# Second layer norm of an adaLN block: normalised rows of groups 1 to 7 on ScalarE instead of GpSimd

## The chip, the core and the metric

The kernel runs on one core of a Trainium2 chip. The core has five instruction streams: TensorE (PE, matmuls and transposes into PSUM banks), VectorE (DVE), ScalarE (ACT), GpSimd (POOL, which cannot read PSUM) and SyncE (SP, which issues the DMAs here). Each runs its own program in order; they wait for one another by semaphores. The metric is device time of one execution in microseconds, the median of several runs.

## The reference

One transformer block on x of 2 x 2048 rows of 512, in float32:

```python
h = _layernorm(x) * (1 + ca) + sa
x = x + ga * attn(h)          # 16 heads, linear attention: elu(q)+1, elu(k)+1, o_w
h = _layernorm(x) * (1 + cb) + sb
x = x + gb * ffn(h)           # gate, up: 512 -> 1376, silu(gate) * up, down: 1376 -> 512
```

with `_layernorm(x) = (x - mean) / sqrt(var + 1e-5)` over the 512 columns; ca, sa, ga, cb, sb, gb come from a small modulation product, and the three weights of the feed-forward part are looked up in a table of 16 values by index matrices. The part that the change touches is the second `_layernorm(x)`.

## The kernel before, in words

The 4096 rows are cut into 8 groups of 512 (4 tiles of 128 rows). Every large product runs as three float16 matmuls on a high and a low part of each operand (the helper `three`, lines 1128 to 1130).

The first half (to about 400 us) runs the first layer norm, the projections and the key-value sums over all groups. The second half is `stage_b(s)` for s = 0 to 7, on each engine in its own function of that name. Stage s runs the gate and up products of the feed-forward part, one chunk (slot) of 128 of the 1376 columns after the other: 9 slots in stage 0, 11 in stage 1, 13 in stage 2, 11 later. Between the slots it runs the attention output and the second layer norm of group n = s + 1, and it starts the attention of group n + 1. After stage 7 come the down products (from about 960 us), which don't concern us.

One slot goes round all engines: TensorE's gate matmuls (12), ScalarE's `silu_gate` (line 707), TensorE's up matmuls (12), VectorE's `hid_full` (line 1062, needs silu and up), ScalarE's `hid_hi` (line 714, the float16 high part), GpSimd's `hid_lo` (line 539, the low part), and a DMA to memory. TensorE's gate of a slot waits for the silu of two slots before, its up for the `hid_full` of two slots before.

The second layer norm of group n: `x1_tile` on VectorE adds the attention output and takes the statistics of a tile; GpSimd's `xn_b` waits for the four statistics and computes 1/sqrt(var + eps) and -mean/sqrt(var + eps) in four short instructions (`norm`, lines 454 to 460), then the normalised rows of the four tiles (line 511) into `xn2`, part of the tile called arena; TensorE transposes them (`t_piece`, line 1136); ScalarE's `h_b` scales and shifts the result into h2 (lines 583, 584), and GpSimd's `h_lo_b` (line 516) makes its low part. Group 0 of the second norm runs in the first half, with its own tile.

The attention of group n + 1 needs a denominator: TensorE's `z_sum` (line 1249), ScalarE's `den` (line 655, a copy of the bank to `kb_row`), VectorE's `rec` (line 1002, the reciprocal), TensorE's `z_spread` (line 1266), VectorE's `qn_full` (line 1009).

The order of all this is written out by hand: each engine's `stage_b` has two tables, `before` and `after`, that say what runs ahead of and behind the slot's own instruction (on ScalarE ahead of and behind `hid_hi`, on GpSimd of `hid_lo`, on VectorE of `hid_full`). VectorE also runs the table lookups of the weights (lines 885 to 893) in the gaps, up to stage 5.

The semaphores that matter: `nmr2_done` counts GpSimd's chain, `xn2_done` the normalised rows (SyncE's `x_next` and TensorE's `t_piece` wait for it), `x2T_done` the transposes.

Of the kernel before, what the change touches and what calls it, by code (L numbers as in the profile page):

```python
# [26 lines left out]
ACT = mybir.ActivationFunctionType  # L27
# [15 lines left out]
TILES = GROUP // P  # L43
# [51 lines left out]
def adaln_kernel(nc, x, qwT, qb, kwT, kb, vwT, vb, owT, ob, lut, gateT, upT, downT, cT, wmod, out):  # L95
    with ExitStack() as ctx:
        def sb(name, shape, dt):
            return ctx.enter_context(nc.sbuf_tensor(name, shape, dt))
# [4 lines left out]
        def part(arena, start, dt, *dims):  # L103

            n = 1
            for d in dims:
                n *= d
            words = n * (2 if dt == F16 else 4) // 4
            v = arena[:, start:start + words]
            if dt != U32:  # L110
                v = v.bitcast(dt)
            if len(dims) == 2:
                v = v.rearrange("p (a b) -> p a b", a=dims[0])
            elif len(dims) == 3:
                v = v.rearrange("p (a b c) -> p a b c", a=dims[0], b=dims[1])
            elif len(dims) == 4:
                v = v.rearrange("p (a b c d) -> p a b c d", a=dims[0], b=dims[1], c=dims[2])
            return v
# [10 lines left out]
        xn2 = part(arena, 2 * tile_w, F32, TILES, HID)  # L129
# [19 lines left out]
        xg = sb("xg", [P, 2, TILES, HID], F32)  # L149
# [49 lines left out]
        ve, rstd, nmr, half, qb_col, qb_neg = (sc[:, SC_ALL + i * TILES:SC_ALL + (i + 1) * TILES] for i in range(6))  # L199
# [11 lines left out]
        def sems(names):  # L211
            return (sem(n) for n in names.split())
# [27 lines left out]
        o_done, xob_done, x1_done, stats2_raw, stats2_done, ve2_done, rstd2_done, nmr2_done, xn2_done = sems(  # L240
            "o_done xob_done x1_done stats2_raw stats2_done ve2_done rstd2_done nmr2_done xn2_done")
        x2T_done, h2_f_done, h2_done = sems("x2T_done h2_f_done h2_done")
# [30 lines left out]
        def wait_apart(eng, s, n):  # L273

            eng.wait_ge(s, n)
            eng.sem_inc(waited, 1)

        def run(extra, at):

            for piece in extra.get(at, ()):  # L280
                piece()
# [158 lines left out]
        def _(pool):  # L440
# [10 lines left out]
            def norm(n, ready, s_ve, s_rstd, s_nmr):  # L451

                wait_apart(pool, ready, 4 * n + 4)
                pool.tensor_scalar(ve, mv[:, :, 1], 1.0, LN_EPS, ALU.mult, ALU.add).then_inc(s_ve, 1)  # L454
                pool.wait_ge(s_ve, n + 1)
                pool.tensor_tensor(rstd, ve, half, ALU.pow).then_inc(s_rstd, 1)
                wait_apart(pool, s_rstd, n + 1)
                pool.tensor_scalar(nmr, mv[:, :, 0], -1.0, 0.0, ALU.mult, ALU.add).then_inc(s_nmr, 1)
                pool.wait_ge(s_nmr, 2 * n + 3)
                pool.tensor_tensor(nmr, nmr, rstd, ALU.mult).then_inc(s_nmr, 1)  # L460
                wait_apart(pool, s_nmr, 2 * n + 4)
# [43 lines left out]

            def xn_b(n, par, rows):
                wait_apart(pool, xn_done, 4 * GROUPS)
                norm(n, stats2_done, ve2_done, rstd2_done, nmr2_done)
                wait_apart(pool, x2T_done, 4 * n + 4)
                for t in range(TILES):  # L510
                    pool.tensor_scalar(rows[:, t], xg[:, par, t], rstd[:, t:t + 1], nmr[:, t:t + 1],
                                       ALU.mult, ALU.add).then_inc(xn2_done, 1)
# [14 lines left out]
            for g in range(6):  # L527
                stage_a(g, g % 2, True, {4: [clear_tail]} if g == 1 else {})

            stage_a(6, 0, True, {2: [lambda: xob(0, 0)], 6: [lambda: qn_lo(0, 0), lambda: qn_lo(0, 1)],  # L530
                                 7: [lambda: qn_lo(0, 2), lambda: qn_lo(0, 3)]}, M_LATE)
            stage_a(7, 1, False, {7: [lambda: xn_b(0, 0, xn2_of[0])]})
            for c in range(KC):
                h_lo_b(0, c)
# [32 lines left out]
            for g in range(GROUPS):  # L567
                par = g % 2
# [7 lines left out]
        def _(act):  # L576
# [4 lines left out]
            def h_chunk(dst, c, h_f_sem, scale, bias):  # L581

                act.activation(dst[:, 0, c], bank[c % 2][:], ACT.Identity, bias=bias, scale=scale)  # L583
                act.activation(h_f[:, c % 2], bank[c % 2][:], ACT.Identity, bias=bias, scale=scale).then_inc(h_f_sem, 1)  # L584
# [56 lines left out]
            def qs_all(n):  # L641
                q = q_of[n]
                act.wait_ge(q_in, 16 * (n + 1))
                for c in range(KC):
                    act.activation(q[:, c], q[:, c], ACT.Copy,
                                   scale=ksq[:, bass.ds(n // PER_BATCH, 1), c]).then_inc(qs_done, 1)

            def den(n):

                act.wait_ge(z_done, n + 1)  # L650
                if n == 1:
                    act.wait_ge(k_read, 4 * GROUPS)
                elif n:
                    act.wait_ge(spread_done, 4 * n)
                act.activation(z_rec[n], bank[6 if n else 1][:], ACT.Copy, bias=ATTN_EPS / SEQ).then_inc(z_read, 1)

            def qn_hi(n, c):
                act.wait_ge(qn_f_done, 4 * n + c + 1)
                if c == 0:
                    act.wait_ge(o_done, 4 * n + 4)  # L660
                act.activation(qn[:, 0, c], qn_f[:, c % 2], ACT.Copy).then_inc(qn_hi_done, 1)

            def h_b(n, c):
                b = n // PER_BATCH
                act.wait_ge(x2T_done, 4 * n + c + 5)
                act.wait_ge(h2_done, 4 * n + c + 3)
                if c == 0 and n >= H2S:
                    act.wait_ge(up_done, SLOT[(n - H2S, FC - 1)] + 1)
                h_chunk(h2[n % H2S], c, h2_f_done, modm[:, 2, c, bass.ds(b, 1)], modm[:, 3, c, bass.ds(b, 1)])
# [11 lines left out]
            for t in range(TILES):  # L681
                act.activation(xg[:, 0, t], xg[:, 0, t], ACT.Identity, bias=nmr[:, t:t + 1],
                               scale=rstd[:, t:t + 1]).then_inc(xn_done, 1)
# [15 lines left out]
            for c in range(KC):  # L699
                h_b(0, c)  # L700

            def silu_gate(e, j):
                m = rows_of(j)
                act.wait_ge(gate_done, e + 1)
                if e >= 2:
                    act.wait_ge(hid_f_done, e - 1)
                act.activation(silu_g[0:m, e % 2], bank[2 + 2 * (e % 2)][0:m], ACT.Silu, scale=c1(C_INV_G)[0:m]).then_inc(silu_g_done, 1)  # L707

            def hid_hi(e, j):
                m = rows_of(j)  # L710
                act.wait_ge(hid_f_done, e + 1)
                if e >= HIDS:
                    act.wait_ge(hid_out[e % HIDS], 16 * (e // HIDS))
                act.activation(hid[0:m, e % HIDS, 0], hid_f[0:m, e % 2], ACT.Copy).then_inc(hid_hi_done, 1)  # L714

            def stage_b(s):
                n = s + 1
                if s == 0:
                    before = {0: [lambda: den(1)], 2: [lambda: qn_hi(1, 0), lambda: qn_hi(1, 1)], 3: [lambda: qn_hi(1, 2), lambda: qn_hi(1, 3)],
                              6: [lambda: den(2)], 7: [lambda: h_b(1, 0), lambda: qn_hi(2, 0), lambda: qn_hi(2, 1)], 8: [lambda: h_b(1, 2)]}  # L720
                    after = {3: [lambda: qs_all(2)], 7: [lambda: h_b(1, 1)], 8: [lambda: h_b(1, 3), lambda: qn_hi(2, 2), lambda: qn_hi(2, 3)]}
                else:
                    before = {6: [lambda: h_b(n, 0)], 7: [lambda: h_b(n, 2)]}
                    after = {6: [lambda: h_b(n, 1)], 7: [lambda: h_b(n, 3)]}
                    if n + 1 < GROUPS:
                        before[1] = [lambda: qs_all(n + 1)]
                        before[4] = [lambda: den(n + 1)]
                        before[6] = [lambda: qn_hi(n + 1, 0), lambda: qn_hi(n + 1, 1), lambda: h_b(n, 0)]
                        before[7] = [lambda: qn_hi(n + 1, 2), lambda: qn_hi(n + 1, 3), lambda: h_b(n, 2)]
                for i, (g, j) in enumerate(STAGES[s]):  # L730
                    silu_gate(SLOT[(g, j)], j)
                    if n < GROUPS:
                        run(before, i)
                    hid_hi(SLOT[(g, j)], j)
                    if n < GROUPS:
                        run(after, i)

            for s in range(GROUPS):
                stage_b(s)
# [742 lines left out]
```

## Time and profile before

| | us |
|---|---|
| median of 3 timed runs | 1248.17 (1248.15 to 1250.17) |
| profiled execution | 1245.79 |
| its span, first to last instruction | 1244.0 |
| TensorE busy | 1163.0 (93%) |
| VectorE busy | 751.4 (60%) |
| ScalarE busy | 392.9 (32%) |
| GpSimd busy | 353.8 (28%) |
| mean granted TensorE clock | 0.979 of 2.4 GHz |

A row of a timeline reads: start, duration, engine, line, operation, output and inputs, shapes, how many in a row; in brackets how long the engine was idle before it and who ended that. Matmuls overlap: one of 512 columns is shown as 0.38 us, and the next starts 0.22 us behind it at 2.4 GHz and 0.43 us behind it at 1.2 GHz. The end of a run of matmuls is taken here as the last start plus 0.38 us.

### The profile page before, as it was taken

What the parts mean: (1) busy time and instruction counts of PE and PEld (TensorE: products, weight loads), DVE (VectorE), ACT (ScalarE), POOL (GpSimd) and SP (SyncE); (2) the same over time, 40 slices, a digit from 0 to 9 for tenths busy, and PEclk for the clock granted to TensorE, in tenths of its full rate; (3) what the DMA queues carried; (4) which work ended last, traced back from release to release, by engine and by line L of the source; (5) the groups of instructions that cost most, each with busy time, mean ns of one, the idle gap of its engine ahead of it and who ended that gap; (6) DMA issues with size and microseconds to landing.
All of it is one profiled execution on the core that took longest, in us unless ns stands there. A gap on an engine that the chain in (4) does not pass through costs nothing.

```text
span 1244.0 us, 14205 instructions
## 1 busy us (share of the span) xinstructions
PE 1163.0 (93%) x5462; PEld 543.5 (44%) x5462; DVE 751.4 (60%) x1105; ACT 392.9 (32%) x609; POOL 353.8 (28%) x337
## 2 busy tenths in 40 slices
PE   4689998899997987999999999999999999999998
PEld 1244444445544333444444444444444444444443
DVE  6897999998565478787786997957411110001000
ACT  3245556456546313242242432324142200000000
POOL 3101000000303426254372563726242211111211
PEclk8799999999999998999999999999999999999999
DMA  9902211221121441121221223112121324444441
GB/s 324 283 2 68 81 48 55 102 68 32 71 68 41 163 169 66 69 92 48 102 76 49 94 74 111 68 74 77 53 98 50 142 106 159 159 159 159 169 151 65
DMA packets 52229, 125.79 MB, mean 101 GB/s; under 512 B 5216, under 2 KB 15456, under 8 KB 47040
## 3 DMA queue, kind: packets, MB, share of 16 engines
q1 hardware_dynamic: 52160, 124.87, 28.9%
q8 instruction: 43, 0.70, 0.2%
q14 instruction: 26, 0.21, 0.1%
HBM read 77.15 MB, written 47.71 MB: 100 GB/s over the span
## 4 chain that ended last, share of the span: by engine, by line
PE 76%; DVE 12%; issue 6%; ACT 4%; POOL 1%; DMA 1%; SPq 0%; POOLq 0%; DVEq 0%; ACTq 0%
PE bank L1128 23%; PE bank L1129 23%; PE bank L1130 23%; DVE look_buf L893 3%; PE bank L1190 2%; PE bank L1136 1%; PE bank L1266 1%; DVE w_ffn L893 1%; PE bank L1308 1%; DMA w_ffn<-in_wmod 1%; ACT h L583 1%; DVE look_buf L890 1%; ACT h_f L584 1%; DVE shared L912 1%; PE bank L1249 1%
## 5 line engine op out<-in xcount | busy, mean ns | idle before, releaser
L1128 PE MATMUL bank<-h,w_ffn 128*128 128x512 f16 (+1 forms) x528 | 203.4, 385 | 13.9 <-POOL h L516 11.4
L1129 PE MATMUL bank<-h,w_ffn 128*128 128x512 f16 (+1 forms) x528 | 203.0, 385 | 0.0
L1130 PE MATMUL bank<-h,w_ffn 128*128 128x512 f16 (+1 forms) x528 | 202.8, 384 | 0.0
L539 POOL TENSOR_TENSOR shared<-hid_f,shared 128x512 f16<-128x512 f32 (+1 forms) x88 | 111.3, 1265 | 318.0 <-ACT shared L714 318.0
L1062 DVE SCALAR_TENSOR_TENSOR hid_f<-bank,sc,shared 128x512 f32<-128x512 f32 (+1 forms) x88 | 65.8, 748 | 150.2 <-PE bank L1130 114.9
L1069 DVE SCALAR_TENSOR_TENSOR shared<-bank,sc,gb_row 128x512 f32<-128x512 f32 x32 | 24.0, 751 | 215.6 <-PE bank L1130 215.6
L1128 PE MATMUL bank<-w_ffn 128*128 128x512 f16 (+1 forms) x352 | 136.3, 387 | 0.9 <-DVE hid_f L1062 0.9
L714 ACT ACTIVATE shared<-hid_f 128x512 f16<-128x512 f32 (+1 forms) x88 | 55.4, 630 | 257.4 <-DVE hid_f L1062 257.4
L1129 PE MATMUL bank<-w_ffn 128*128 128x512 f16 (+1 forms) x352 | 136.2, 387 | 0.0
L1130 PE MATMUL bank<-w_ffn 128*128 128x512 f16 (+1 forms) x352 | 136.2, 387 | 0.0
L1128 PE MATMUL bank<-arena,h 128*128 128x512 f16 x256 | 98.9, 386 | 6.6 <-issue 3.1
L707 ACT ACTIVATE shared<-bank,sc 128x512 f32<-128x512 f32 (+1 forms) x88 | 60.3, 685 | 130.4 <-PE bank L1130 130.3
L1130 PE MATMUL bank<-arena,h 128*128 128x512 f16 x256 | 98.8, 386 | 0.0
L1129 PE MATMUL bank<-arena,h 128*128 128x512 f16 x256 | 98.7, 385 | 0.0
L890 DVE TENSOR_SCALAR look_buf<-look_buf,tab_x,tab 128x512 uint32<-128x512 uint32 x133 | 97.7, 764 | 0.8
L572 POOL TENSOR_TENSOR xg<-xg,shared 128x512 f32<-128x512 f32 x32 | 40.9, 1278 | 198.2 <-DVE shared L1069 198.2
L1128 PEld LDWEIGHTS bank<-h,w_ffn 128*128 128x128 f16 (+1 forms) x528 | 53.5, 101 | 85.3 <-issue 17.8
L454 POOL TENSOR_SCALAR sc<-mv 128x4 f32<-128x4 f32 x16 | 5.5, 342 | 266.0 <-DVE mv L812 223.1
L1130 PEld LDWEIGHTS bank<-h,w_ffn 128*128 128x128 f16 (+1 forms) x528 | 53.6, 102 | 62.9 <-issue 3.3
L1129 PEld LDWEIGHTS bank<-h,w_ffn 128*128 128x128 f16 (+1 forms) x528 | 53.6, 101 | 59.0 <-issue 2.9
L893 DVE COPY_PREDICATED look_buf<-look_buf 128x512 uint32<-128x512 uint32 x76 | 73.2, 963 | 1.1
L1128 PE MATMUL bank<-arena,w_ffn 128*128 128x512 f16 (+1 forms) x176 | 66.8, 379 | 0.0
(189 smaller groups left out, 1994.3 us busy)
## 6 DMA issues: line engine op xcount, KB each, us to landing
hid_dram<-shared SPq DMA_DIRECT2D x80, 256.0 KB, 2.0
w_ffn<-hid_dram SPq DMA_DIRECT2D x8, 2560.0 KB, 9.6
xg<-in_x SPq DMA_DIRECT2D x16, 1024.0 KB, 6.9
qp_dram<-qp SPq DMA_DIRECT2D x8, 1024.0 KB, 4.9
x_dram<-xg SPq DMA_DIRECT2D x8, 1024.0 KB, 4.0
xg<-x_dram SPq DMA_DIRECT2D x8, 1024.0 KB, 5.0
out<-xg SPq DMA_DIRECT2D x7, 1024.0 KB, 11.1
qp<-qp_dram SPq DMA_DIRECT2D x6, 1024.0 KB, 5.2
```

Of the source, the lines that this page charges most:

```text
L539: pool.tensor_tensor(hid[0:m, e % HIDS, 1], hid_f[0:m, e % 2], hid[0:m, e % HIDS, 0], ALU.subtract).then_inc(hid_done, 1)
L572: pool.tensor_tensor(xg[:, par, t], xg[:, par, t], y_t[:, t % 2], ALU.add).then_inc(y_done, 1)
L707: act.activation(silu_g[0:m, e % 2], bank[2 + 2 * (e % 2)][0:m], ACT.Silu, scale=c1(C_INV_G)[0:m]).then_inc(silu_g_done, 1)
L714: act.activation(hid[0:m, e % HIDS, 0], hid_f[0:m, e % 2], ACT.Copy).then_inc(hid_hi_done, 1)
L890: ins = dve.tensor_scalar(buf(dst), buf("m0"), tab_x[:, a:a + 1], tab[:, 2 * a:2 * a + 1], ALU.bitwise_and, ALU.bitwise_xor)
L893: ins = dve.copy_predicated(buf(dst), buf(a), buf(b))
L1062: dve.scalar_tensor_tensor(hid_f[0:m, i], bank[3 + 2 * i][0:m], c1(C_HID)[0:m], silu_g[0:m, i], ALU.mult, ALU.mult).then_inc(hid_f_done, 1)
L1069: dve.scalar_tensor_tensor(y_t[:, t % 2], bank[2 + t][:], c1(C_INV_D), gb_row[:, g // PER_BATCH], ALU.mult, ALU.mult).then_inc(y_read, 1)
L1128: pe.matmul(dst, a_hi, b_hi, start=first, stop=False)
L1129: pe.matmul(dst, a_hi, b_lo, start=False, stop=False)
L1130: last = pe.matmul(dst, a_lo, b_hi, start=False, stop=end)
L1190: last = pe.matmul(bank[6 + c // 2][:, at:at + n], kp[:, t % 2, c * P:(c + 1) * P], v_one[:, t % 2, c], start=(t == 0 and c % 2 == 0), sto ...
```

## The change

The rows of groups 1 to 7 are no longer computed by GpSimd behind its `norm`, but by ScalarE, as activations with the function Identity, rstd as scale and nmr as bias. GpSimd keeps `norm` for all groups, and keeps the rows of group 0. ScalarE's new function waits for the chain (`nmr2_done`) and for the transposes of the group before (`x2T_done`). In stage 0 it stands behind `hid_hi` of slot 5, where GpSimd's stood behind `hid_lo` of slot 5. In stages 1 to 6 it stands behind `hid_hi` of slot 4; GpSimd's chain stays behind `hid_lo` of slot 3. GpSimd waits, ahead of `norm`, until ScalarE has read the factors of the group before.

```diff
@@ gpsimd
             def xn_b(n, par, rows):
                 wait_apart(pool, xn_done, 4 * GROUPS)
+                wait_apart(pool, xn2_done, 4 * n)
                 norm(n, stats2_done, ve2_done, rstd2_done, nmr2_done)
+                if n:
+                    return
                 wait_apart(pool, x2T_done, 4 * n + 4)
                 for t in range(TILES):
                     pool.tensor_scalar(rows[:, t], xg[:, par, t], rstd[:, t:t + 1], nmr[:, t:t + 1],
@@ scalar
+            def xn_b(n, par, rows):
+                act.wait_ge(nmr2_done, 2 * n + 4)
+                act.wait_ge(x2T_done, 4 * n + 4)
+                for t in range(TILES):
+                    act.activation(rows[:, t], xg[:, par, t], ACT.Identity, bias=nmr[:, t:t + 1], scale=rstd[:, t:t + 1]).then_inc(xn2_done, 1)
@@ scalar, stage_b, s == 0
-                    after = {3: [lambda: qs_all(2)], 7: [lambda: h_b(1, 1)], 8: [lambda: h_b(1, 3), lambda: qn_hi(2, 2), lambda: qn_hi(2, 3)]}
+                    after = {3: [lambda: qs_all(2)], 5: [lambda: xn_b(1, 1, xn2)], 7: [lambda: h_b(1, 1)], 8: [lambda: h_b(1, 3), lambda: qn_hi(2, 2), lambda: qn_hi(2, 3)]}
@@ scalar, stage_b, s > 0
-                    after = {6: [lambda: h_b(n, 1)], 7: [lambda: h_b(n, 3)]}
+                    after = {4: [lambda: xn_b(n, n % 2, xn2)], 6: [lambda: h_b(n, 1)], 7: [lambda: h_b(n, 3)]}
```

ScalarE's program around group 1 (stage 0, from the copy `hid_hi` of slot 5 on; `kb_row<-bank` is the denominator copy of group 2), before:

```order
L714 ACTIVATE shared<-hid_f 128x512
L707 ACTIVATE shared<-bank,sc 128x512
L655 ACTIVATE kb_row<-bank 128x512
L714 ACTIVATE shared<-hid_f 128x512
L707 ACTIVATE shared<-bank,sc 128x512
```

and with the change (the lines are numbered on; L723 is `hid_hi`, L716 the silu, L658 the denominator copy):

```order
L723 ACTIVATE shared<-hid_f 128x512
L670 ACTIVATE arena<-xg,sc 128x512 x4
L716 ACTIVATE shared<-bank,sc 128x512
L658 ACTIVATE kb_row<-bank 128x512
L723 ACTIVATE shared<-hid_f 128x512
L716 ACTIVATE shared<-bank,sc 128x512
```

The four rows stand ahead of the silu of slot 6 and of the denominator copy. In stages 1 to 6 the denominator copy stands ahead of the copy of slot 4; the piece of stage 2 before:

```order
L707 ACTIVATE shared<-bank,sc 128x512
L655 ACTIVATE kb_row<-bank 128x512
L714 ACTIVATE shared<-hid_f 128x512
L707 ACTIVATE shared<-bank,sc 128x512
L714 ACTIVATE shared<-hid_f 128x512
```

and with the change:

```order
L716 ACTIVATE shared<-bank,sc 128x512
L658 ACTIVATE kb_row<-bank 128x512
L723 ACTIVATE shared<-hid_f 128x512
L670 ACTIVATE arena<-xg,sc 128x512 x4
L716 ACTIVATE shared<-bank,sc 128x512
L723 ACTIVATE shared<-hid_f 128x512
```

Only the silu of slot 5 and what follows it stand behind the four rows there.

## Rows read from the trace of the kernel before

**Rows 1.** The page: busy us, share of the span and instructions of each engine.

```profile
PE 1163.0 (93%) x5462; PEld 543.5 (44%) x5462; DVE 751.4 (60%) x1105; ACT 392.9 (32%) x609; POOL 353.8 (28%) x337
```

**Rows 2.** Waits of TensorE, 380 to 960 us: total, times, longest, in us.

```profile
PE bank L1128 <- POOL h L516: 11.4, 2, 8.4
PE bank L1266 <- DVE kb_row L1002: 4.2, 1, 4.2
```

**Rows 3.** Busy time in a stretch: length, PE, PEld, DVE, ACT, POOL, clock, DMA.

```profile
571.00:960.00 389.00, 389.00 (x1844) 181.56 (x1843) 265.34 (x358) 126.20 (x198) 173.38 (x153) 1.00 0.21 75
```

**Rows 4.** VectorE in order of time, group 1: hidden product of slot 6, reciprocal.

```profile
459.53 0.75 DVE L1062 SCALAR_TENSOR_TENSOR hid_f<-bank,sc,shared 128x512 f32<-128x512 f32 x1 [2.89 <-issue]
460.19 3.34 DVE L1002 RECIPROCAL kb_row<-kb_row 128x512 f32<-128x512 f32 x1
```

**Rows 5.** TensorE in order of time around the two holes of stage 0.

```profile
459.05 0.38 PE L1130 MATMUL bank<-h,w_ffn 128*128 128x512 f16 x1
463.59 1.45 PE L1266 MATMUL bank<-kb_row,head_out 32*128 32x512 f32 x4 [4.16 <-DVE kb_row L1002]
...
488.12 0.61 PE L1128 MATMUL bank<-h,w_ffn 128*128 128x512 f16 x1 [8.38 <-POOL h L516]
```

**Rows 6.** ScalarE in order of time: silu of slot 6, denominator copy.

```profile
456.88 0.69 ACT L707 ACTIVATE shared<-bank,sc 128x512 f32<-128x512 f32 x1 [2.22 <-PE bank L1130]
457.47 0.59 ACT L655 ACTIVATE kb_row<-bank 128x512 f32<-128x512 f32 x1
```

**Rows 7.** Line 511, the rows on GpSimd: ns minimum, median, maximum; starts.

```profile
L511 POOL TENSOR_SCALAR arena<-xg,sc x28: 767/772/776, 458.5 to 912.1; 128x512 f32<-128x512 f32 x28
```

**Rows 8.** GpSimd's release, ScalarE's rows of the first norm, its query scalings.

```profile
325.20 0.20 POOL L460 TENSOR_TENSOR sc<-sc 128x4 f32<-128x4 f32 x1
...
325.43 2.93 ACT L623 ACTIVATE xg<-xg,sc 128x512 f32<-128x512 f32 x4 [7.61 <-POOL sc L460]
328.26 0.67 ACT L597 ACTIVATE shared<-bank,sc 128x512 f32<-128x512 f32 x1
...
L623 ACT ACTIVATE xg<-xg,sc x28: 797/800/815, 57.8 to 327.6; 128x512 f32<-128x512 f32 x28
...
432.38 2.54 ACT L645 ACTIVATE qp<-qp,ksq 128x512 f32<-128x512 f32 x4
```

**Rows 9.** GpSimd in order of time, group 1: end of the chain, the rows.

```profile
457.99 0.20 POOL L460 TENSOR_TENSOR sc<-sc 128x4 f32<-128x4 f32 x1
458.50 3.03 POOL L511 TENSOR_SCALAR arena<-xg,sc 128x512 f32<-128x512 f32 x4 [0.31 <-POOL sc L460]
```

**Rows 10.** Busy time and granted clock (third value from the end), as rows 3.

```profile
464.27:467.68 3.41, 3.41 (x11) 1.04 (x8) 3.16 (x7) 0.00 (x0) 0.00 (x0) 0.50 0.90 293
467.68:471.09 3.41, 3.41 (x20) 1.77 (x18) 2.08 (x4) 2.00 (x4) 0.00 (x0) 1.00 0.05 17
...
484.75:488.16 3.41, 0.04 (x1) 0.04 (x2) 3.34 (x3) 1.60 (x3) 3.41 (x4) 0.50 0.82 339
488.16:491.57 3.41, 3.41 (x9) 1.21 (x10) 3.34 (x4) 0.00 (x0) 3.41 (x3) 0.50 0.00 0
```

**Rows 11.** Group 3 in order of time: VectorE, ScalarE and TensorE from slot 4 on.

```profile
611.27 3.34 DVE L1002 RECIPROCAL kb_row<-kb_row 128x512 f32<-128x512 f32 x1
...
611.39 0.63 ACT L714 ACTIVATE shared<-hid_f 128x512 f16<-128x512 f32 x1 [2.91 <-DVE hid_f L1062]
613.14 0.69 ACT L707 ACTIVATE shared<-bank,sc 128x512 f32<-128x512 f32 x1 [1.12 <-PE bank L1130]
...
616.68 0.74 DVE L1062 SCALAR_TENSOR_TENSOR hid_f<-bank,sc,shared 128x512 f32<-128x512 f32 x1
...
619.28 0.60 PE L1136 MATMUL bank<-ident,arena 128*128 128x128 f32 x4
```

**Rows 12.** Group 7 in order of time: ScalarE's copy of slot 4, VectorE's product.

```profile
910.73 0.63 ACT L714 ACTIVATE shared<-hid_f 128x512 f16<-128x512 f32 x1 [2.75 <-DVE hid_f L1062]
...
915.12 0.75 DVE L1062 SCALAR_TENSOR_TENSOR hid_f<-bank,sc,shared 128x512 f32<-128x512 f32 x1 [4.43 <-PE bank L1130]
```

## The prediction

> **What bounds the kernel now.** I read four views, from the whole to the place. The page first: TensorE is busy 93% of the span and no other engine is over 60%, so the time is TensorE's stream plus the holes in it [rows 1]. Then the waits of TensorE in the stretch where the changed work runs, 380 to 960 us. The reader is to see that none of them names the normalised rows of the second layer norm: the largest are 11.4 us for GpSimd's low part of h2 (one of 8.4 us) and 4.2 us for VectorE's reciprocal [rows 2]. Third, the busy time by stretches: from 571 to 960 us TensorE is busy 389.00 of 389.00 us, so groups 3 to 7 of the second half run with no hole at all, and only groups 1 and 2 lie where TensorE sometimes waits [rows 3]. Last, the instructions in order of time at group 1, where the 4.2 us hole is. Its chain: the reciprocal of group 2's denominators starts on VectorE when the hidden product of slot 6 is out (459.53 us) and runs 460.19 to 463.53; TensorE, done at 459.05 + 0.38 = 459.43, starts the spreading matmuls at 463.59 [rows 4, 5].
>
> What feeds that reciprocal is ScalarE's copy of the denominators, kb_row, which ran 457.47 to 458.06 right behind the silu of slot 6 at 456.88 [rows 6]. Both were early: the silu was out at 457.57, the copy at 458.06, and VectorE took neither until 459.53 and 460.19. So ScalarE has about 2 us of cover at this place, and the change puts work in front of exactly these two instructions.
>
> **The change, part by part.** Removed: 28 GpSimd instructions (groups 1 to 7, four each), 767 to 776 ns each [rows 7], 28 x 0.77 = 21.6 us of GpSimd. Nobody on TensorE waited for them, so by themselves they are worth nothing on the path.
>
> Added on ScalarE: the same 28 tiles. No row shows ScalarE writing this tile, but the first layer norm's rows are the same function with the same operands: four in 2.93 us, the next instruction starting 0.10 us before their end [rows 8]. The lower bound is the four query scalings, which take one such operand less, 2.54 us [rows 8]; the upper is four of 0.80 us [rows 8] without overlap, 3.2 us. I take 2.93. No table is loaded for them: Identity runs between Silus in this half already, and the new order has no table load at the place.
>
> Added as a wait: ScalarE stands still until the square root chain on GpSimd is through. The release costs next to nothing: GpSimd's last instruction ended at 325.40 and ScalarE began at 325.43 [rows 8]. What is queued behind the waiting instructions are the silu of the next slot and, in group 1, the denominator copy.
>
> *Group 1 (stage 0, behind slot 5).* The chain's last instruction ends at 457.99 + 0.20 = 458.19 [rows 9]. GpSimd gets one more wait ahead of the chain, for a count reached long before; I give it 0.03 us. ScalarE starts at 458.25 and, 2.93 us on, ends at 461.18. The silu of slot 6 runs 461.08 to 461.77 (0.69), the denominator copy 461.67 to 462.26 (0.59). VectorE's hidden product starts at 461.80 instead of 459.53, and the reciprocal 0.66 us behind it at 462.46 instead of 460.19; the copy, out at 462.26, no longer matters by 0.2 us. Reciprocal out at 465.80, TensorE at 465.86 instead of 463.59: the hole grows by 2.27 us, from 4.16 to 6.43. With the bounds of the four rows it would be 1.9 to 2.5. This adds to the end in full: behind it TensorE's second matmul group of slot 7 releases the VectorE chain that sets the 8.4 us hole (8.38 us up to 488.12, so from 479.74 [rows 5]), so that hole moves along and does not shrink. TensorE's transposes of group 1 come behind that hole and the next matmul group, and get their rows at 461.2 against 458.50 + 3.03 = 461.5 before [rows 9].
>
> *The clock behind the hole.* TensorE was granted 1.2 GHz from 464.27 to 467.68 after the 4.16 us hole, and from 484.75 to 491.57 around and after the 8.4 us hole; otherwise 2.4 GHz here [rows 10]. So the low stretch was 3.4 us for the one and 6.8 for the other. The work done at the low level was 3.41 us before, which lost 1.7 us. The new hole begins at the same time, so the low stretch again starts at 464.27; TensorE comes back at 465.86. If the stretch ends at 467.68, 1.8 us are worked at half speed and 0.9 lost: 0.8 us is given back. If it is twice as long, as behind the 8.4 us hole, it ends at 471.09, 5.2 us are worked at half speed and 2.6 lost: 0.9 us more. Bounds -0.8 and +0.9. The new hole of 6.43 us stands nearer to 8.38 (1.95 off) than to 4.16 (2.27 off), so I take +0.9.
>
> The Trainium skill ("TensorE: Matmul & The Clock Gate", section "What's actually happening") says that the gate is free-running and does not restart with a kernel, so the point at which it falls varies from run to run. By this rule some runs would get the one end and some the other; the three times of before lie 2.0 us apart, which agrees but does not show it.
>
> *Groups 2 to 6 (slot 4).* Here the chain sits behind slot 3's low part, and ScalarE comes to the new rows only behind the copy of slot 4. In group 3 that copy runs 611.39 to 612.02, and GpSimd has its own rows under way by then, so the chain is ready. The four rows take 611.93 to 614.86, the silu then ends at 615.45 instead of 613.83. VectorE takes that silu at 616.68, since it is in the reciprocal and lookups until then: hidden by 1.2 us. The transposes want the rows at 619.28 and have them 4.4 us ahead [rows 11]. The denominator copy stands in front of the new rows here, so the reciprocal is not touched. In group 7 the margin is smallest: copy out at 911.36, rows until 914.2, silu until 914.8, VectorE's product at 915.12 [rows 12]. Cost 0, and even a late silu would have TensorE's next two matmul groups (12 matmuls each, 2.6 us) as cover. GpSimd's low part of slot 4 goes out 1 us earlier and the load of the next x group 1.7 us later; nothing waits for either for another stage.
>
> Sum: 2.27 + 0.9 = +3.2 us. Against the profiled execution: 1245.79 + 3.2 = 1249.0 us, and its span from 1244.0 to 1247.2. The median of the timed runs, 1248.17, stands 2.4 us above the profiled one, as runs of the same kernel do here; 1248.17 + 3.2 = 1251.4 us.
>
> **The rivals.**
>
> *A, the hole grows but the clock gives back.* The same 2.27 with -0.8: +1.5 us, 1249.7. For it: the low stretch behind the hole nearest in place ended at 467.68. Against: the hole is half as long again.
>
> *B, the cover holds: no change.* It needs the silu of slot 6 and the copy in time for 459.5 and 460.2, so the new rows would have to be over by 458.9. They cannot start before 458.2, and four rows take 2.5 at least. Only if the profile's starts on GpSimd, which are rough, lay 2 us late. Time 1248.2.
>
> *C, faster: VectorE is relieved.* In groups 1 and 2 VectorE sets TensorE's holes, and 4 x 0.77 us of GpSimd reads go away beside it, in each. If VectorE had been held for all of them, 2 x 3.0 = 6.0 us would be free, and with the 3.2 of the sum -2.8: 1245.4. Against: beside GpSimd's rows in group 1 VectorE had a product of 0.75 us and a reciprocal of 3.34 us, and in group 3 the reciprocal beside other work is 3.34 too [rows 4, 11]; nothing was stretched.
> The Trainium skill ("SBUF — State Buffer", section "Who interferes with whom") has a port pair that GpSimd and VectorE lock for a whole instruction, while ScalarE has its own. By that rule moving rows to ScalarE can only help VectorE; the trace shows no stretched VectorE instruction at these rows, so here it would free nothing.
>
> *D, slower in every group.* If ScalarE's rows with their wait took 1.2 us more than reckoned, the silu of slot 5 would hold VectorE in groups 2 to 7, and with it GpSimd's and ScalarE's work for the next transposes. At 0.5 us in each of six groups: 3.2 + 3.0 = +6.2 us, 1254.4. It decides from a row time of about 1.03 us; the nearest rows say 0.80, and TensorE's lead hides a late product.
>
> **How the numbers follow.** Forecast (+3.2) 0.50, A (+1.5) 0.27, B (0) 0.10, C (-2.8) 0.05, D (+6.2) 0.08. 0.2% is 2.5 us, about what a measurement of this kernel can tell from no change. The forecast's own range is 1250.2 to 1252.6, by the row bounds (-0.4, +0.3) and another 0.9 us for where the clock falls at the two later holes. Some 0.05 of the forecast's 0.50 and all but 0.02 of A fall under 2.5 us: slower 0.45 + 0.02 + 0.08 = 0.55, the same 0.39, faster 0.06. The range from B to just short of D, 1248.0 to 1253.3, leaves out C, D and a little of the tails.
>
> **What would show it.** In the profile after: 28 ScalarE rows of about 0.80 us on the new line, the first at 458.3; TensorE's wait for the reciprocal at 6.4 us instead of 4.2, ending at 465.9; a low clock until 471.1 rather than 467.7; the first matmul group behind that hole ending 3 us later; the 8.4 us hole unchanged in length; TensorE full from some 574 to 963 us. The sum is wrong if the reciprocal still starts at 460.2, if another wait appears in the transposes of stages 1 to 6, or if VectorE's products of slot 5 start on a wait for ScalarE.

## The result and the profile after

| | before | after |
|---|---|---|
| median of 20 runs, us | 1246.72 (1244.85 to 1250.17) | 1249.76 (1248.04 to 1251.88) |
| profiled execution, us | 1245.79 | 1249.74 |
| its span, us | 1244.0 | 1247.9 |
| ScalarE busy, us | 392.9 | 412.1 |
| GpSimd busy, us | 353.8 | 332.5 |

The changed kernel is slower: the ratio is 1.0027, 95% interval 1.0020 to 1.0033, so 3.0 us by the medians, with an interval of 2.5 to 4.1 us. +3.2 was forecast. The median of before over more runs is 1.45 us lower than that of the three runs that were shown, so 1249.76 stands 1.6 us under the 1251.4 of the forecast though the difference agrees. It is also below the forecast's own range (1250.2 to 1252.6) and at the time that rival A named; only the difference tells them apart, and A's +1.5 us lies outside the interval.

First the waits of TensorE, 380 to 964 us, of the changed kernel (total, times, longest, in us); they answer to [rows 2]:

```profile
PE bank L1137 <- POOL h L519: 11.7, 2, 8.4
PE bank L1275 <- DVE kb_row L1011: 6.4, 1, 6.4
```

The wait for the reciprocal has grown from 4.2 to 6.4 us; the longest single wait is 8.4 us as before. The place in order of time, one engine after the other (GpSimd, ScalarE, VectorE, TensorE), for [rows 4 to 6] and [rows 9]:

```profile
457.11 0.20 POOL L460 TENSOR_TENSOR sc<-sc 128x4 f32<-128x4 f32 x1
...
457.35 2.93 ACT L670 ACTIVATE arena<-xg,sc 128x512 f32<-128x512 f32 x4 [3.57 <-POOL sc L460]
460.18 0.67 ACT L716 ACTIVATE shared<-bank,sc 128x512 f32<-128x512 f32 x1
460.75 0.58 ACT L658 ACTIVATE kb_row<-bank 128x512 f32<-128x512 f32 x1
...
460.88 0.75 DVE L1071 SCALAR_TENSOR_TENSOR hid_f<-bank,sc,shared 128x512 f32<-128x512 f32 x1 [5.13 <-ACT shared L716]
461.55 3.34 DVE L1011 RECIPROCAL kb_row<-kb_row 128x512 f32<-128x512 f32 x1
...
458.17 0.38 PE L1139 MATMUL bank<-h,w_ffn 128*128 128x512 f16 x1
464.94 2.07 PE L1275 MATMUL bank<-kb_row,head_out 32*128 32x512 f32 x4 [6.39 <-DVE kb_row L1011]
...
491.35 0.61 PE L1137 MATMUL bank<-h,w_ffn 128*128 128x512 f16 x1 [8.37 <-POOL h L519]
```

What to read: ScalarE begins its rows 0.04 us behind the chain's end and takes 2.93 us for the four. The silu of slot 6 comes out at 460.85, and VectorE's hidden product, which in the kernel before began 0.10 us behind TensorE's last up matmul, now waits for this silu (5.13 us idle, released by L716). The reciprocal follows, and TensorE behind it. TensorE reached the hole 0.88 us earlier in this execution (458.55 for 459.43) and left it 1.35 us later. The early arrival was there before the first moved row began at 457.35: a lookup of VectorE stands at 453.82 for 454.70.

The clock, for [rows 10]; the granted clock, as a share of 2.4 GHz, is the third value from the end:

```profile
461.97:465.39 3.42, 0.45 (x2) 0.45 (x4) 3.38 (x3) 0.32 (x1) 1.15 (x1) 0.50 0.38 92
465.39:468.80 3.41, 3.41 (x9) 0.78 (x8) 3.16 (x7) 0.00 (x0) 0.00 (x0) 0.50 0.83 288
468.80:472.21 3.41, 3.41 (x10) 1.27 (x8) 2.32 (x4) 0.00 (x0) 0.00 (x0) 0.50 0.03 8
472.21:475.63 3.42, 3.42 (x21) 1.93 (x19) 0.20 (x1) 3.06 (x5) 0.00 (x0) 1.00 0.00 0
```

The level is 1.2 GHz from 461.97 to 472.21. TensorE worked 7.27 us of that (464.94 on), against 3.41 us of work at the low level before. The second hole is the 8.4 us one, which ends at 491.35; behind it the level is low to 496.10, 4.75 us of work against 3.45. The 3.9 us by which the span grew are then: arrival -0.88, hole +2.23 (6.39 - 4.16), from its end to the second hole's end +1.88 (26.41 us against 24.53), behind that +0.7.

Group 3, group 7 and the stretch without holes, for [rows 11], [rows 12] and [rows 3]: first in order of time, ScalarE and then VectorE in each group, then the busy time of the stretch:

```profile
615.83 2.92 ACT L670 ACTIVATE arena<-xg,sc 128x512 f32<-128x512 f32 x4
618.65 0.67 ACT L716 ACTIVATE shared<-bank,sc 128x512 f32<-128x512 f32 x1
...
620.58 0.75 DVE L1071 SCALAR_TENSOR_TENSOR hid_f<-bank,sc,shared 128x512 f32<-128x512 f32 x1
...
917.98 0.67 ACT L716 ACTIVATE shared<-bank,sc 128x512 f32<-128x512 f32 x1
...
919.02 0.75 DVE L1071 SCALAR_TENSOR_TENSOR hid_f<-bank,sc,shared 128x512 f32<-128x512 f32 x1 [4.43 <-PE bank L1139]
```
```profile
574.00:963.00 389.00, 389.00 (x1842) 181.76 (x1841) 265.37 (x360) 139.39 (x218) 157.91 (x132) 1.00 0.21 76
```

The silu of slot 5 is out 1.3 us before VectorE takes it in group 3 and 0.37 us before in group 7, and TensorE has no hole in 389 us. VectorE's busy time in that stretch is 265.37 us against 265.34 before.

### The profile page after: what moved, and what is told of

It is laid out like the page before. It is cut to its first block, busy times and chain, and to the rows that moved or that the text cites. A ratio compares the mean times of both kernels' runs of the same rounds, so it can differ in the third digit from the quotient of the medians.

```text
span 1247.9 us, 14213 instructions
## 1 busy us (share of the span) xinstructions
PE 1165.0 (93%) x5462; PEld 544.5 (44%) x5462; DVE 750.0 (60%) x1105; ACT 412.1 (33%) x637; POOL 332.5 (27%) x309
## 4 chain that ended last, share of the span: by engine, by line
PE 75%; DVE 12%; issue 6%; ACT 4%; POOL 1%; DMA 1%; SPq 0%; POOLq 0%; DVEq 0%; ACTq 0%
PE bank L1137 23%; PE bank L1138 23%; PE bank L1139 23%; DVE look_buf L902 3%; PE bank L1199 2%; PE bank L1145 1%; PE bank L1275 1%; PE bank L1317 1%; DVE w_ffn L902 1%; DMA w_ffn<-in_wmod 1%; DVE look_buf L899 1%; ACT h L586 1%; ACT h_f L587 1%; DVE shared L921 1%; PE bank L1258 1%
## 5 line engine op out<-in xcount | busy, mean ns | idle before, releaser
L723 ACT ACTIVATE shared<-hid_f 128x512 f16<-128x512 f32 (+1 forms) x88 | 55.4, 630 | 247.9 <-DVE hid_f L1071 247.9
L716 ACT ACTIVATE shared<-bank,sc 128x512 f32<-128x512 f32 (+1 forms) x88 | 60.1, 683 | 120.8 <-PE bank L1139 120.8
```

## The experiments

Each was timed beside the kernel before on the same chip. The theory is that all of the loss comes from the two instructions that group 1's four rows were put in front of: the silu of slot 6 and the denominator copy. "Whole change" is the changed kernel; diffs are against it unless said. A ratio is to the kernel before, with its 95% interval in brackets.

**Group 1 alone.**

```diff
@@ gpsimd xn_b
-                if n:
+                if n == 1:
@@ scalar stage_b, s > 0
-                    after = {4: [lambda: xn_b(n, n % 2, xn2)], 6: [lambda: h_b(n, 1)], ...
+                    after = {6: [lambda: h_b(n, 1)], ...
```

> Only group 1's rows on ScalarE; groups 2 to 7 stay on GpSimd. Theory (the loss is group 1's place, ahead of the silu of slot 6 and the denominator copy): TensorE's wait for the reciprocal is 6.4 us as with the whole change, and the time is the whole change's, +3 us (+0.24%). Rival 1 (each group adds a little): about 3/7 of a us per group, so +0.4 us and a wait of 4.2 us plus little. Rival 2 (the loss is the clock at other holes, moved by chance): anywhere within 1.5 us of before.

Measured: 1249.81 us against 1246.17, ratio 1.0028 (1.0019 to 1.0037); TensorE's wait 6.38 us. The four rows of group 1 alone give the loss of the whole change (1.0027).

**Groups 2 to 7 alone.** The edit's counterpart: `if n > 1: return` on GpSimd, and ScalarE's entry of stage 0 removed.

> Groups 2 to 7 on ScalarE, group 1 on GpSimd. Theory: no change from before (within 0.5 us), TensorE's wait for the reciprocal 4.2 us, TensorE without a hole from about 571 to 960 us. Rival 1 (each group adds a little): +2.6 us. Rival 3 (VectorE is relieved where GpSimd's rows are gone): faster than before by up to 3 us, to be seen in a shorter wait in stage 1.

Measured: 1246.31 us against 1246.17, ratio 1.0003 (0.9994 to 1.0012); the wait is 4.16 us and TensorE is busy 385.00 of 385.00 us from 575 to 960. 24 of the 28 rows cost nothing that can be measured, and taking them off GpSimd wins nothing that can be measured either; the interval is -0.7 to +1.5 us. That is too wide for the "within 0.5 us" of the expectation, but it excludes rival 1's +2.6 us and rival 3's gain of anything over 0.7 us.

**All 28 rows on ScalarE, group 1's one slot later.**

```diff
-                    after = {3: [lambda: qs_all(2)], 5: [lambda: xn_b(1, 1, xn2)], 7: ...
+                    after = {3: [lambda: qs_all(2)], 6: [lambda: xn_b(1, 1, xn2)], 7: ...
```

> The whole change, but in stage 0 the four rows stand behind the copy of slot 6 instead of slot 5. Theory: the silu of slot 6 and the denominator copy are in time again, the reciprocal starts behind the hidden product as before, TensorE waits 4.2 us, the time is that of before (+0.0, within 0.5 us), though ScalarE runs all 28 rows; the transposes of group 1 get their rows at about 464.5, 4 us ahead. Rival (the rows themselves or their wait cost, wherever they stand): +3 us, with a wait of the transposes of group 1.

Measured: ratio 1.0002 (0.9993 to 1.0010); the wait is 4.16 us. The work is the same as in the whole change, and most or all of the loss is gone, so it is the place. The rows are out at 463.89 and TensorE transposes them from 470.23 on, without a wait. The medians, 1247.44 and 1246.17, lie 1.3 us apart, more than the ratio, and the interval reaches to +1.2 us; a small rest is not excluded. Its profiled execution shows one reason for such scatter. The hole is as long as in the kernel before, but the low clock behind it lasts to 469.61:

```profile
459.37:462.78 3.41, 0.20 (x1) 0.00 (x0) 3.12 (x2) 2.33 (x4) 1.16 (x1) 1.00 0.19 77
462.78:466.20 3.42, 2.47 (x6) 0.70 (x7) 3.28 (x6) 1.11 (x2) 0.00 (x0) 0.50 0.48 159
466.20:469.61 3.41, 3.41 (x10) 1.20 (x9) 3.26 (x7) 0.00 (x0) 0.00 (x0) 0.50 0.61 229
469.61:473.02 3.41, 3.41 (x19) 1.81 (x18) 0.27 (x1) 2.59 (x5) 0.00 (x0) 1.00 0.00 0
```

From the end of this hole to the end of the next are 25.71 us (463.73 to 489.44), against 24.53 before, where the low level lasted 3.4 us, and 24.54 with groups 2 to 7 alone, whose hole was 4.16 us too.

**Half the dose.** Tiles 2 and 3 of group 1 stay on GpSimd.

```diff
@@ gpsimd xn_b
-                if n:
+                if n > 1:
                     return
-                for t in range(TILES):
+                for t in range(2 if n == 1 else 0, TILES):
@@ scalar xn_b
-                for t in range(TILES):
+                for t in range(2 if n == 1 else TILES):
```

> The whole change, but of group 1's four tiles two stay on GpSimd. Theory: ScalarE is through 2 x 0.71 = 1.4 us earlier, so TensorE's wait is 6.4 - 1.4 = 5.0 us, and the time lies between before and the whole change, +0.8 us for the hole and up to 0.9 us more or less for the clock: +0.8 to +1.7. Rival (it is the wait for the chain, not the rows, that delays ScalarE): the wait stays near 6.4 us and the time at +3.

Measured: ratio 1.0018 (1.0009 to 1.0027), 1248.69 against 1246.17. The wait came out as expected, TensorE in order of time:

```profile
463.26 2.08 PE L1275 MATMUL bank<-kb_row,head_out 32*128 32x512 f32 x4 [4.97 <-DVE kb_row L1011]
488.65 0.61 PE L1137 MATMUL bank<-h,w_ffn 128*128 128x512 f16 x1 [8.37 <-POOL h L519]
```

The hole grew by 0.81 us, the time by about 2.2 to 2.5, more than the 0.8 to 1.7 expected. The interval, 1.1 to 3.4 us, holds the upper end; from the hole's end to the next hole's are 25.39 us, 0.86 more than before. The wait of 4.97 us rules out the rival, by which it would have stayed near 6.4. The dose shows in the hole as reckoned; the time can't be told from that of the whole change, whose interval overlaps.

**The hole filled, on the kernel before and on the changed one.** Only the clock is to change.

```diff
@@ tensor z_spread, in the kernel before; range(27) in the changed one
+                if n == 2 and c == 0:
+                    pe.wait_ge(qn_f_done, 4 * n - 1)
+                    for i in range(17):
+                        pe.matmul(bank[7][:], h[:, 0, 0, 0, 0:P], h[:, 0, 0, 0], start=True, stop=True)
                 if c == 0:
                     pe.wait_ge(rec_done, n + 1)
```

> The kernel before, with 17 matmuls of 512 columns (3.7 us, result unused) put into the 4.2 us hole of stage 0, so that only the clock is changed. Theory (the half-speed work behind the hole costs some 1.7 us): the first matmuls behind the hole run at 2.4 GHz (0.22 us apart), the wait itself ends at the same time, and the kernel is 1.7 us faster than before (-0.14%). Rival (the clock costs nothing, since VectorE sets the next hole's end): no change.

> The changed kernel, with 27 matmuls of 512 columns (5.8 us, result unused) in its 6.4 us hole. Theory: the clock stays at 2.4 GHz behind it, 2.6 to 3.6 us of half-speed loss go, and what is left against the filled kernel before is the hole's growth alone, 2.2 to 2.3 us. So about +0.5 us against before (-1.7 + 2.2). Rival (the growth of the hole is not what costs): filled kernels equal.

Measured: 1243.94 and 1246.29 us against 1246.72, ratios 0.9975 (0.9957 to 0.9994) and 0.9990 (0.9981 to 1.0000). TensorE in order of time, first before filled, then the changed one filled:

```profile
463.70 1.13 PE L1270 MATMUL bank<-kb_row,head_out 32*128 32x512 f32 x4 [0.49 <-DVE kb_row L1002]
486.58 0.61 PE L1128 MATMUL bank<-h,w_ffn 128*128 128x512 f16 x1 [8.37 <-POOL h L516]
```
```profile
465.38 1.13 PE L1279 MATMUL bank<-kb_row,head_out 32*128 32x512 f32 x4 [0.56 <-DVE kb_row L1011]
488.25 0.61 PE L1137 MATMUL bank<-h,w_ffn 128*128 128x512 f16 x1 [8.36 <-POOL h L519]
```

The clock is full from 455 to 475 us in both (1.00), the spreading matmuls take 1.13 us instead of 1.45 and 2.07, and from the end of this hole to the end of the next it is 22.88 and 22.87 us: the same for both. So the clock behind this hole cost 1.65 us in the profile of before (24.53) and 3.54 us in that of the changed kernel (26.41). The filled kernels are 2.35 us apart by their medians, near the hole's growth of 2.2 to 2.3, but their intervals against before, -5.4 to -0.7 us and -2.4 to 0.0 us, overlap. Before gained 2.8 us by the medians, not 1.7; the interval holds both, and the 1.7 was taken from an execution with the shorter of the two low stretches seen behind a 4.16 us hole. The changed kernel, filled, came out at -0.4 us against before by the medians where +0.5 was expected; its interval excludes +0.5, so this expectation missed, by about what before gained over its own.

**The reciprocal early.** Denominator copy of group 2 behind slot 5's copy, its reciprocal ahead of slot 6's product; on the kernel before and on the changed one, where the copy stands ahead of the four rows. The diff is that of the changed kernel; on the kernel before ScalarE's new entry is `5: [lambda: den(2)]` alone. The comments name the table.

```diff
@@ scalar stage_b, s == 0
-                              6: [lambda: den(2)], 7: ...
-                    after = {3: [lambda: qs_all(2)], 5: [lambda: xn_b(1, 1, xn2)], 7: ...
+                              7: ...
+                    after = {3: [lambda: qs_all(2)], 5: [lambda: den(2), lambda: xn_b(1, 1, xn2)], 7: ...
@@ vector stage_b, s == 0
-                              7: [lambda: qn_full(2, 0), ...     # table `before`
+                              6: [lambda: rec(2)], 7: [lambda: qn_full(2, 0), ...
-                             4: [lambda: x1_tile(1, 1, 2)], 6: [lambda: rec(2)]}     # table `after`
+                             4: [lambda: x1_tile(1, 1, 2)]}
```

> The kernel before, with the denominator copy of group 2 behind the copy of slot 5 on ScalarE and its reciprocal ahead of the hidden product of slot 6 on VectorE. Theory: the reciprocal starts when VectorE is through with its lookups (about 456.7) and is out at 460.0; TensorE's wait falls from 4.2 to about 0.6 us and the clock stays up: -3.6 - 1.7 = -5.3 us (-0.4%), if the VectorE chain behind it moves along in full. Rival (VectorE's lookups and products set the next hole anyway): -3.3 us or less, the 8.4 us hole grows by what was won.

> The changed kernel, with the denominator copy of group 2 ahead of the four new rows on ScalarE and its reciprocal ahead of the hidden product of slot 6. Theory: the reciprocal no longer depends on what stands behind the new rows, and the change costs nothing any more: TensorE's wait about 0.6 us and the time that of the kernel before with the same edit (within 0.5 us). Rival (the late silu of slot 6 alone costs): 1 us or more slower than that, since the hidden product of slot 6 comes at about 461.8 instead of 460.0.

Measured: 1241.84 and 1242.93 us against 1246.72, ratios 0.9953 (0.9940 to 0.9966) and 0.9963 (0.9950 to 0.9976). The 4.2 us hole is 0.5 us in both. Before gains 4.9 us by the medians and 5.9 by the ratio (interval 4.2 to 7.5); theory said 5.3. In the changed kernel the theory was only partly right: 1.1 us of loss stay, as the rival had it, and its fastest run (1242.58) is slower than the slowest of the other (1242.31). Its VectorE and TensorE in order of time:

```profile
455.63 3.34 DVE L1011 RECIPROCAL kb_row<-kb_row 128x512 f32<-128x512 f32 x1
460.83 0.75 DVE L1071 SCALAR_TENSOR_TENSOR hid_f<-bank,sc,shared 128x512 f32<-128x512 f32 x1 [1.87 <-ACT shared L716]
...
459.02 1.13 PE L1275 MATMUL bank<-kb_row,head_out 32*128 32x512 f32 x4 [0.51 <-DVE kb_row L1011]
468.23 2.67 PE L1275 MATMUL bank<-kb_row,head_out 32*128 32x512 f32 x4 [1.92 <-DVE qn_f L1018]
```

The late silu still holds VectorE 1.87 us; the product, the clamps (lines 874 to 877, which go with the lookups) and lookups behind it, and then the query products (qn_f) come late, and TensorE waits 1.92 us there instead of 0.53. With the first hole closed, VectorE's own chain is next: from the end of the first wait to the end of the second hole it is 25.62 us against 24.19 in the other kernel, though that hole itself is 5.3 us here and 8.5 there. In these two profiles what TensorE lost on the way came out of the hole; what VectorE lost did not.

**The reciprocal early, and group 1's rows behind slot 6.** Edit: `5: [lambda: den(2)], 6: [lambda: xn_b(1, 1, xn2)]`, VectorE as above; beside it the kernel before with the early reciprocal once more.

> All 28 rows on ScalarE, group 1's behind the copy of slot 6, and the early denominator copy and reciprocal of group 2. Theory (only what stands ahead of the silu of slot 6 and of the copy costs): the time of the kernel before with the early reciprocal, -4.9 to -5.9 us (-0.4 to -0.5%) against before, within 0.5 us of it. Rival 1 (ScalarE's rows still cost 1 us, as in the changed kernel with the early reciprocal): -3.8 us. Rival 2 (the clamp on VectorE ran beside GpSimd's rows and was stretched, 0.68 + 0.88 us for 0.42 + 0.43, so without GpSimd's rows it is relieved): the clamp's first two instructions take 0.42 and 0.43 us and the kernel is up to 0.7 us faster than before with the early reciprocal.

> The kernel before with the early denominator copy and reciprocal once more, on the same chip as the one with ScalarE's rows behind slot 6, for the comparison of the two. Theory: -4.9 to -5.9 us against before, equal to the other within 0.5 us. Rival (relief of VectorE): 0.7 us slower than the other.

Measured: 1241.10 and 1241.49 us against 1246.43, ratios 0.9953 (0.9938 to 0.9968) and 0.9959 (0.9946 to 0.9972). Both beat the kernel before, and with it the changed one, by 0.4 to 0.5%, and can't be told from each other. Rival 1 falls: its -3.8 us lies just outside the interval (-7.7 to -4.0). Of rival 2 the durations are right. The profiles show a gain up to the next hole: from the end of the first wait to that hole's end are 23.56 us (459.76 to 483.32), against 24.19 in both profiled executions of the kernel before with the early reciprocal. A gain in the time of the whole isn't shown (0.4 us by the medians, the runs overlap). The four rows end at 463.76, and TensorE's first transpose waits 0.2 us for them, so the place behind slot 6 has no cover left in this kernel.

## Why the prediction was right

- **Cover of about 2 us at group 1.** Right. With the rows behind slot 6 the loss is gone within the interval; with them ahead of slot 6's silu VectorE waits for the silu and no longer for TensorE.
- **Rows of 2.93 us, release of 0.03.** 2.93 and 0.04 us measured; half the rows took 1.52.
- **Hole +2.27.** Right. +2.23 in the profile, +2.22 with group 1 alone. The silu decided and not the denominator copy, which was out at 461.33, 0.2 us before VectorE took it, as worked out.
- **Clock +0.9.** The sign was right and the size was too small: this term was mis-sized. In the profile it was 1.88 us behind this hole and 0.7 behind the next, where I had put nothing into the sum. Group 1 alone gives the same, 26.30 us from hole's end to hole's end. The low level began at 461.97 and not at 464.27: that it would begin where it did before was the wrong assumption, since with one and the same hole of 4.16 us it began at 464.27 in one kernel and at 462.78 in another. By the medians the clock's share is what the filled kernels leave, 3.04 - 2.35 = 0.7 us, but these medians are too uncertain to call that near to 0.9. Part of the agreement of +3.2 with the measured +3.0 is luck: in the profile hole and clock together came to 4.8 us, and an arrival 0.88 us earlier, which no term of the sum had, took some of it back.
- **What the clock was weighed by.** The new hole's nearness to 8.38 us chose the longer low stretch. The low level did last longer behind it, but behind one of three 4.16 us holes it lasted 6.8 us too, so the length of the hole alone did not decide it. The working of the range gives 1250.1 at its lower end, for the 1250.2 written.
- **Groups 2 to 7 at 0.** Right as far as can be measured: ratio 1.0003 alone. The margins were put at 1.2 us in group 3 and 0.3 in group 7; the trace has 1.3 and 0.37.
- **The 8.4 us hole moves along.** Right, 8.37 us. It is set by VectorE's chain, which starts from TensorE's own matmuls. The transposes of group 1 come ahead of this hole and behind the one that grew, at 468.89 before and 472.05 after, with the rows ready at 461.5 and 460.3.
- **Rivals.** A (the clock gives back) came in neither profile with a 6.4 us hole. The interval, 2.5 to 4.1 us, leaves out A (+1.5), B (0), C (-2.8) and D (+6.2).

## What to carry to other kernels

Moving work to an engine that is idle for two thirds of the time can cost more than it moves, if the new place stands ahead of an instruction with less cover than the work is long: read, at every place where it is repeated, when the instructions behind it were taken, not how idle the engine is. Here 24 of 28 moved instructions cost nothing that could be measured and 4 cost 3 us. Where a wait is bound by instructions that could run in an earlier gap, move those first: here a copy and a reciprocal gave 4.9 us, and no placing of the 28 rows gave anything that could be measured.

## What the runs showed of the hardware

A hole of TensorE cost more than its length here, and by an amount that the length did not fix: behind equal holes of 4.16 us the low clock lasted 3.4 us in one execution and 6.8 in another, 1.2 us of time. Those are two kernels with one execution each, but the runs of one kernel differ too: over 33 runs of the kernel before the mean granted clock was 0.975 to 0.982 and the time 1244.8 to 1250.2 us.

VectorE's instructions took longer beside GpSimd's. In the kernel before with the early reciprocal the clamp's first instructions ran beside GpSimd's rows (458.15 to 461.34), and in the kernel with the rows on ScalarE beside nothing on GpSimd until 461.01; VectorE in order of time, the two kernels in this order:

```profile
460.03 0.68 DVE L865 TENSOR_SCALAR shared<-ga_row 128x512 f32<-128x512 f32 x1
460.74 0.88 DVE L866 TENSOR_SCALAR shared<-ga_row 128x512 uint32<-128x512 uint32 x1
```
```profile
460.20 0.41 DVE L874 TENSOR_SCALAR shared<-ga_row 128x512 f32<-128x512 f32 x1
460.64 0.43 DVE L875 TENSOR_SCALAR shared<-ga_row 128x512 uint32<-128x512 uint32 x1
```

They take 0.68 and 0.88 us for 0.41 and 0.43. The Trainium skill ("SBUF — State Buffer", section "Who interferes with whom") says that a VectorE `tensor_scalar` in a two-port mode and a GpSimd instruction lock each other out of a shared port pair, while ScalarE has its own; these four rows agree. In the kernel before, VectorE ran only a product and the reciprocal beside group 1's rows, neither of them longer than elsewhere, so the change had nothing to win there.

GpSimd's rows are the smaller part of this. In the kernel before, the same two instructions of the clamp, first with nothing on GpSimd and then, one slot later, beside its low parts (all in order of time, the last four of both engines):

```profile
464.31 0.43 DVE L867 TENSOR_SCALAR shared<-shared 128x512 f32<-128x512 f32 x1
464.77 0.69 DVE L868 SCALAR_TENSOR_TENSOR ga_row<-shared 128x512 f32<-128x512 f32 x1
...
473.68 1.16 POOL L539 TENSOR_TENSOR shared<-hid_f,shared 128x512 f16<-128x512 f32 x1 [11.03 <-ACT shared L714]
473.77 1.35 DVE L867 TENSOR_SCALAR shared<-shared 128x512 f32<-128x512 f32 x1
474.79 2.90 POOL L498 TENSOR_TENSOR qn<-qn_f,qn 128x512 f16<-128x512 f32 x2
475.15 1.53 DVE L868 SCALAR_TENSOR_TENSOR gb_row<-shared 128x512 f32<-128x512 f32 x1
```

The lookups behind them follow suit: two of line 890 take 2.56 us for 1.00, one of line 893 takes 1.70 for 0.72. Together that is 4.3 us in the chain of VectorE that sets the 8.4 us hole (the chain that ended last runs through these instructions from 472.19 to 482.66), against 0.7 us for the two stretched instructions beside the rows. No run took the low parts away, so what that would win isn't shown.
